# The first attention's context: halves made as rows, stored, and turned by the load from memory instead of by TensorE

## What is computed

```python
x = x + attention(layernorm(x), ctx)
def attention(query, ctx):
    q = query @ w_q.T + b_q
    k = ctx @ w_k.T + b_k
    v = ctx @ w_v.T + b_v
    scores = einsum('bhqd,bhkd->bhqk', q, k) / sqrt(16)
    y = einsum('bhqk,bhkd->bhqd', softmax(scores), v)
    return y @ w_o.T + b_o
```

## Time and profile before

| | us |
|---|---|
| median of 3 runs | 3887.06 (3885.37 to 3891.0) |
| the profiled execution | 3889.76 |
| its span in the profile | 3888.0 |
| TensorE busy | 3699.7 (95%) |
| VectorE busy | 3091.1 (80%) |
| ScalarE busy | 2208.8 (57%) |
| GpSimd busy | 2208.9 (57%) |
| first attention | from 23 to about 900 |
| granted clock over the span | 0.979 of 2.4 GHz |

### The profile page before, as it was taken

One profiled execution on the slowest core, in us unless ns is written; L12 is line 12 of the kernel. 1 busy time (PEld: TensorE's weight loads), 2 busy tenths in 40 slices (PEclk: granted clock), 3 DMA queues, 4 the chain that ended last, 5 costly groups with the idle time before them and its releaser, 6 DMA issues. The chain is left out here.

```text
span 3888.0 us, 134428 instructions
## 1 busy us (share of the span) xinstructions
PE 3699.7 (95%) x47408; PEld 2875.9 (74%) x47408; DVE 3091.1 (80%) x5266; ACT 2208.8 (57%) x4529; POOL 2208.9 (57%) x3316
## 2 busy tenths in 40 slices
PE   5999999994899999999999996899999989999999
PEld 4777777772677777777777775566666658888888
DVE  4888888886777777777777775799889877777777
ACT  3777777775444444444444442577767764555554
POOL 5666666663354533333333334366656667887777
PEclk9999999997899999999999998899999999999999
DMA  4677777765333322222222223699999962333332
GB/s 123 187 210 206 211 213 219 215 201 160 99 81 80 81 66 74 65 74 65 67 71 65 74 62 87 157 211 212 219 209 209 213 151 80 79 75 76 79 75 72
DMA packets 834241, 502.59 MB, mean 129 GB/s; under 512 B 262037, under 2 KB 824408, under 8 KB 833480
## 3 DMA queue, kind: packets, MB, share of 16 engines
q1 hardware_dynamic: 832680, 493.49, 50.3%
q0 software_dynamic: 928, 0.49, 0.1%
HBM read 251.27 MB, written 214.96 MB: 120 GB/s over the span
## 5 line engine op out<-in xcount | busy, mean ns | idle before, releaser
L1506 ACT ACTIVATE all_region<-phase_loop_hid,phase_b1T 128x128 f32<-128x128 f32 x2048 | 586.1, 368 | 728.0 <-PE phase_loop_hid L193 693.5
L191 PE MATMUL phase_loop_hid<-phase_loop_moe_h,phase_w_hi 128*128 128x128 f16 x4096 | 728.1, 220 | 0.1
L193 PE MATMUL phase_loop_hid<-phase_loop_moe_h,phase_w_lo 128*128 128x128 f16 x4096 | 726.4, 219 | 0.0
L192 PE MATMUL phase_loop_hid<-phase_loop_moe_h,phase_w_hi 128*128 128x128 f16 x4096 | 726.4, 219 | 0.0
L1112 DVE TENSOR_REDUCE phase_loop_mx<-phase_loop_score 128x8 f32<-128x1024 f32 x512 | 625.8, 1222 | 100.6 <-PE phase_loop_score L875 94.8
L1472 PE MATMUL phase_loop_moe_y<-phase_w,all_region 128*128 x2048 | 693.6, 379 | 0.3
L1030 ACT ACTIVATE phase_loop_pt<-phase_loop_scoreT 128x1024 f32<-128x1024 f32 x448 | 458.6, 1024 | 271.5 <-PE phase_loop_scoreT L909 269.2
L1474 PE MATMUL phase_loop_moe_y<-phase_w,all_region 128*128 x2048 | 558.2, 273 | 0.0
L1524 DVE TENSOR_SCALAR all_region<-all_region 128x512 f16<-128x512 f32 x512 | 257.6, 503 | 248.6 <-PE phase_loop_moe_y L1474 192.8
L191 PEld LDWEIGHTS phase_loop_hid<-phase_loop_moe_h,phase_w_hi 128*128 x4096 | 400.6, 98 | 66.5 <-issue 0.4
L1527 DVE SCALAR_TENSOR_TENSOR all_region<-all_region 128x512 f16<-128x512 f32 x512 | 410.1, 801 | 17.6
(11 more groups left out here) (276 smaller groups left out, 9846.6 us busy)
## 6 DMA issues: line engine op xcount, KB each, us to landing
qk_scratch<-phase_loop_qk SPq DMA_DIRECT2D x192, 256.0 KB, 3.5
phase_loop_qS<-qk_scratch SPq DMA_DIRECT2D x768, 64.0 KB, 3.2
phase_loop_cin<-in_ctx SPq DMA_DIRECT2D x128, 256.0 KB, 4.6
x_scratch<-phase_loop_x SPq DMA_DIRECT2D x128, 256.0 KB, 3.1
h_scratch<-phase_loop_hr SPq DMA_DIRECT2D x128, 256.0 KB, 3.8
phase_loop_kS<-qk_scratch SPq DMA_DIRECT2D x384, 64.0 KB, 2.4
ks_scratch<-ct_scratch SPq DMA_DIRECT2D x384, 64.0 KB, 2.4
phase_loop_kS<-ks_scratch SPq DMA_DIRECT2D x128, 192.0 KB, 3.9
```

The costliest lines, as they stand in the source:

```text
L191: eng.matmul(out, l_hi, r_hi, start=start, stop=False)
L192: eng.matmul(out, l_hi, r_lo, start=False, stop=False)
L193: return eng.matmul(out, l_lo, r_hi, start=False, stop=stop)
L1506: i = act.activation(hf[n % NF][:, j, :], hid(u, n)[:, j * S:(j + 1) * S], ACT.Gelu, bias=w["b1"][:, bass.ds(e * HB + (4 * half + j), 1)], ...
```

## The change

The context is no longer turned by TensorE. `hi_c` and `lo_c` now read `cin` in SBUF and write the halves side by side as rows into a new tile `cr`, of two buffers. `store_cr` writes them to a scratch tensor in memory, 256 KB per unit, and `load_cT` brings them back by one transposing load into `cT`. `kk` waits for that load in place of `lo_c`, and `store_ct` too. `t_c` is gone, from TensorE's list and from the plan of the PSUM bank. All tasks but those of the context get a lag larger by one, so the pipeline is one step deeper (DEPTH 13). In SyncE's list `load_c` and `store_cr` stand first and `load_cT` behind `store_h`.

The diff, cut to its core (the lists of GpSimd and ScalarE change in their lags alone):

```diff
-    DEPTH = 12
+    DEPTH = 13 if first else 12
...
+        cr = first and two("cr", [P, PAIR, 2, D], F16)
...
-            plan = [(3, "t_x"), (8, "t_y"), (3, "q"), (7, "y0"), (2, "t_c"), (3, "k"), (5, "t_max"), (3, "v"),
-                    (7, "y1"), (8, "o")]
-            shared = (("t_x", "y0", "y1"), ("t_y", "t_c", "t_max", "v"), ("q", "k", "o"))
+            plan = [(4, "t_x"), (9, "t_y"), (4, "q"), (8, "y0"), (4, "k"), (6, "t_max"), (4, "v"), (8, "y1"), (9, "o")]
+            shared = (("t_x", "y0", "y1"), ("t_y", "t_max", "v"), ("q", "k", "o"))
...
                 def load_c(u):
-                    (s_tc if first else s_ve).wait(sp, u.back(2))
+                    (s_cl if first else s_ve).wait(sp, u.back(2))
                     d_c.inc(sp.dma_start(cin[u.slot][:, :, :], cv[u.no]), u)
...
+                def store_cr(u):
+                    s_ch.wait(sp, u)
+                    s_cl.wait(sp, u)
+                    d_cr.inc(rows_out(sp, io["cr"][u.no], cr[u.slot][:, :, :, :]), u)
+
+                def load_cT(u):
+                    d_cr.wait(sp, u)
+                    s_k.wait(sp, u.back(2))
+                    s_v.wait(sp, u.back(4))
+                    d_ct.wait(sp, u.back(4))
+                    d_cT.inc(columns_in(sp, cT[u.slot4][:, :, :, :], io["cr"][u.no]), u)
...
                 def store_ct(u):
-
-                    s_cl.wait(sp, u)
-                    s_ch.wait(sp, u)
+                    d_cT.wait(sp, u)
...
-                    tasks = [(5, place_max), (3, stack_k), (2, store_q), (9, store_x1), (0, load_x), (4, store_ct),
-                             (4, store_max), (9, store_h), (0, load_c), (2, store_k), (2, stack_q)]
+                    tasks = [(0, load_c), (1, store_cr), (6, place_max), (4, stack_k), (3, store_q), (10, store_x1), (1, load_x),
+                             (5, store_ct), (5, store_max), (10, store_h), (1, load_cT), (3, store_k), (3, stack_q)]
...
-                def t_c(u):
-                    d_c.wait(pe, u)
-                    free("t_c", u)
-                    transpose_pair(pe, ring["t_c"], cin[u.slot], ident).then_inc(s_tc.sem, 1)
...
                 def kk(u):
-                    s_cl.wait(pe, u)
+                    d_cT.wait(pe, u)
...
                 def vv(u):
-                    s_cl.wait(pe, u)
...
-                    tasks = [(3, make["t_x"]), (8, make["t_y"]), (7, av(2)), (5, score(3)), (7, score_t(3)),
-                             (3, make["q"]), (7, make["y0"]), (2, make["t_c"]), (7, av(3)), (6, score_t(0)),
...
+                    tasks = [(4, make["t_x"]), (9, make["t_y"]), (8, av(2)), (6, score(3)), (8, score_t(3)),
+                             (4, make["q"]), (8, make["y0"]), (8, av(3)), (7, score_t(0)),
...
-                hi_c = first and hi_part(s_ch, ring["t_c"][:, :], cT, s_tc, [(s_v, 4), (d_ct, 4)], p2(CTX_X))
+
+                def hi_c(u):
+
+                    d_c.wait(act, u)
+                    d_cr.wait(act, u.back(2))
+                    act.activation(cr[u.slot][:, :, 0, :], cin[u.slot][:, :, :], ACT.Copy, scale=p2(CTX_X)).then_inc(s_ch.sem, 1)
...
-                lo_c = first and lo_part(s_cl, ring["t_c"][:, :], cT, 0, s_ch, [(s_v, 4), (d_ct, 4)], p2(CTX_X))
+
+                def lo_c(u):
+                    s_ch.wait(v, u)
+                    v.scalar_tensor_tensor(out=cr[u.slot][:, :, 1, :], in0=cin[u.slot][:, :, :], scalar=p2(CTX_X),
+                                           in1=cr[u.slot][:, :, 0, :], op0=ALU.mult, op1=ALU.subtract).then_inc(s_cl.sem, 1)
...
-                             (4, row_max(2)), (2, lo_x), (4, row_max(3)), (7, lo_y), (2, lo_q), (1, norm0_stats),
-                             (1, lo_c), (8, norm1_stats)]
+                             (5, row_max(2)), (3, lo_x), (5, row_max(3)), (8, lo_y), (3, lo_q), (2, norm0_stats),
+                             (1, lo_c), (9, norm1_stats)]
...
+        io["cr"] = nc.dram_tensor("cr_scratch", (n_seq // PAIR, PAIR * S, 2 * D), F16, kind="Internal").ap()
```

More of the change, by code:

```diff
@@ L531, in attention @@
         d_stq, d_stk = k.dsig("d_stq", 6), k.dsig("d_stk", 6 if first else 2)
-        d_ct = k.dsig("d_ct")
+        d_ct, d_cr, d_cT = k.dsig("d_ct"), k.dsig("d_cr"), k.dsig("d_cT")
         g = lambda name, per=1: k.sig(name, per)
-        s_tx, s_tc, s_xh, s_xl, s_ch, s_cl = g("s_tx"), g("s_tc"), g("s_xh"), g("s_xl"), g("s_ch"), g("s_cl")
+        s_tx, s_xh, s_xl, s_ch, s_cl = g("s_tx"), g("s_xh"), g("s_xl"), g("s_ch"), g("s_cl")
         s_q, s_k, s_v, s_qh, s_ql, s_kh, s_kl, s_ve = (g(n) for n in "s_q s_k s_v s_qh s_ql s_kh s_kl s_vev".split())
@@ L552, in attention @@
         read = {"y0": (s_yn, 1), "y1": (s_yn, 2), "t_y": (s_yl, 1), "o": (s_x1, 1), "t_max": (s_mte, 1),
-                "t_x": (s_xl, 1), "q": (s_ql, 1), "k": (s_kl, 1), "v": (s_ve, 1),
-                "t_c": (s_cl, 1)}
+                "t_x": (s_xl, 1), "q": (s_ql, 1), "k": (s_kl, 1), "v": (s_ve, 1)}
         ring, bank_of = {}, {}
@@ L789, in _ @@
                 if first:
-                    tasks = [(6, bias_x), (8, maxima), (5, norm0), (12, rstd1), (12, rows1)]
+                    tasks = [(7, bias_x), (9, maxima), (6, norm0), (13, rstd1), (13, rows1)]
                 else:
@@ L964, in o @@
                     project_rows(u, ring["o"], lambda u: yT[u.slot], "wo").then_inc(s_o.sem, 1)
-                make = {"t_x": t_x, "t_c": t_c, "q": q if first else fold_q, "k": kk, "v": vv, "t_max": t_max,
+                make = {"t_x": t_x, "q": q if first else fold_q, "k": kk, "v": vv, "t_max": t_max,
                         "y0": y_rows(0), "y1": y_rows(1), "t_y": t_y, "o": o}
                 if first:
-                    tasks = [(3, make["t_x"]), (8, make["t_y"]), (7, av(2)), (5, score(3)), (7, score_t(3)),
-                             (3, make["q"]), (7, make["y0"]), (2, make["t_c"]), (7, av(3)), (6, score_t(0)),
-                             (3, make["k"]), (5, make["t_max"]), (6, av(0)), (6, score_t(1)), (4, score(0)),
-                             (3, make["v"]), (7, make["y1"]), (6, score_t(2)), (4, score(1)), (8, make["o"]),
-                             (6, av(1)), (4, score(2))]
+                    tasks = [(4, make["t_x"]), (9, make["t_y"]), (8, av(2)), (6, score(3)), (8, score_t(3)),
+                             (4, make["q"]), (8, make["y0"]), (8, av(3)), (7, score_t(0)),
+                             (4, make["k"]), (6, make["t_max"]), (7, av(0)), (7, score_t(1)), (5, score(0)),
+                             (4, make["v"]), (8, make["y1"]), (7, score_t(2)), (5, score(1)), (9, make["o"]),
+                             (7, av(1)), (5, score(2))]
                 else:
@@ L1052, in _ @@
                 if first:
-                    tasks = [(5, copy_y(0)), (1, hi_x), (6, hi_y), (5, expo(3)), (1, hi_q), (0, hi_c), (5, copy_y(1)),
-                             (4, expo(0)), (3, copy_max), (1, hi_k), (4, expo(1)), (4, expo(2)), (1, copy_v),
-                             (7, norm1)]
+                    tasks = [(6, copy_y(0)), (2, hi_x), (7, hi_y), (6, expo(3)), (2, hi_q), (0, hi_c), (6, copy_y(1)),
+                             (5, expo(0)), (4, copy_max), (2, hi_k), (5, expo(1)), (5, expo(2)), (2, copy_v),
+                             (8, norm1)]
                 else:
@@ L1130, in _ @@
                 if first:
-                    tasks = [(7, norm_y(0)), (3, lo_k), (4, row_max(0)), (7, norm_y(1)), (4, row_max(1)), (8, add_x),
-                             (4, row_max(2)), (2, lo_x), (4, row_max(3)), (7, lo_y), (2, lo_q), (1, norm0_stats),
-                             (1, lo_c), (8, norm1_stats)]
+                    tasks = [(8, norm_y(0)), (4, lo_k), (5, row_max(0)), (8, norm_y(1)), (5, row_max(1)), (9, add_x),
+                             (5, row_max(2)), (3, lo_x), (5, row_max(3)), (8, lo_y), (3, lo_q), (2, norm0_stats),
+                             (1, lo_c), (9, norm1_stats)]
                 else:
```

## The result

The changed kernel takes **4336.16 us** (median of 4 runs, 4327.83 to 4337.39). The kernel before took 3888.39 on the same chip (4 runs, 3885.37 to 3891.0). The ratio is 1.1147 [1.1128, 1.1167]: 448 us slower, inside the range, 64 us under the predicted 4400. The profiled execution took 4327.8 us; its span is 4325.9, with TensorE busy for 3804.7 of it (88%) and VectorE for 3095.4 (72%).

A forecast was written before the change was run, and what follows sets the result against it. TensorE, busy for the whole 13.17 us step, was taken as the bound. A loop of 21.7 us per step gives 58 x (21.7 - 13.17) = 495, plus 12 and 6: +513 us, predicted 4400 us, range 4230 to 4520.

The forecast's parts named there:

- The removal: Four context transposes per unit leave TensorE, 0.53 us x 64 = 34 us; not subtracted because TensorE waits there instead.
- rival C: First attention: TensorE stays the bound and gives back 34 us, less 6 at the start: 3859 us; chance 0.03.
- The loop: First attention, steps 6 to 63: score_t(0), lo_c, store_cr and place_max wait in a circle, 21.7 us per step.
- TensorE from `score_t(0)` to the end of `score(3)`: Loop term: 9.93 us of consecutive TensorE work, plus 2.5 us lost to the low clock after the stop.
- VectorE to the end of `lo_c`: Loop term: row_max(3), lo_y, lo_q, the statistics and lo_c on VectorE, 4.85 us.
- The queue: Loop term on SyncE: waking, issuing store_cr, a gap and the two place_max transfers, 1.23 us.
- Landing of `place_max`: Loop term: from the end of its last issue until it lands, 3.2 us, bounds 1.9 and 4.36.
- the start: First load of x stands behind the context's store and both copies: +6 us once.
- the steps in which only `kS` is in the loop: Steps 4 and 5, before the first place_max: a shorter loop of 19.1 us, costing 6 us each.
- A: First attention: the loop closes but the clock stays up, 19.2 us per step, 4255 us; chance 0.15.
- B: First attention: no loop, but the queue or DMA engines become the bound, 14.2 us per step, 3953 us; chance 0.04.
- D: First attention: low clock through the whole step or landing of 4.4 us, about 4555 us; chance 0.07.

The follow-up runs named there:

- e3: The kernel before without the four transposes, context halves copied straight into cT, no store or load added, context not turned: 3879.81 us against 3883.28.
- e8: The changed kernel with 42 useless matmuls of 256 columns ahead of score_t(0)'s wait for place_max: 4211.21 us.
- e1: The changed kernel with the context's store and transposing load one step later, at the same places of the queue's list: 4006.06 us.
- e12: The changed kernel with the context's store and transposing load issued by ScalarE instead of SyncE's queue: 3979.54 us.
- e11: e1 with store_max and place_max issued by ScalarE instead of SyncE's queue: 3953.95 us.
- e10: e3 with store_max and place_max issued by ScalarE instead of SyncE's queue: 3892.51 us.
- e2: e1 with a plain load of the same 256 KB in place of the transposing one, context not turned: 3934.75 us.

## Why the prediction was right, and where it was off

**What bounds the kernel.** The judgement of the place was right: the slack of about 1 us between `place_max` and TensorE, and what stands in the queue ahead of it. The removal was rightly not subtracted, but its size was wrong even by itself: the 34 us that rival C was built on are 0 in e3. A busy share of 100% was read as the bound, and the next limits lie within 0.3 us of the step (12.95 against 13.17 in e3).

**The loop, term by term**, in the step of 20.48 us shown above:

- TensorE from `score_t(0)` to the end of `score(3)`: forecast 9.93 + 2.5 of low clock. Measured 411.52 - 398.93 = 12.59, so 2.66 of low clock. Confirmed, and by e8 too (at least 2.2 per step).
- VectorE to the end of `lo_c`: forecast 4.85, measured 416.29 - 411.52 = 4.77.
- The queue: forecast 1.23, measured 417.46 - 416.29 = 1.17.
- Landing of `place_max`: forecast 3.2, measured 419.41 - 417.46 = **1.95**. This is the term that was mis-sized. It came from the store of 256 KB ahead of it, taken at the 3.8 us of the like store of h. In the changed kernel that store lands sooner, as these two rows show (DMA issues from 200 to 1200: count, KB each, median us to landing):

```profile
cr_scratch<-phase_loop_cr SPq DMA_DIRECT2D x49, 256.0 KB, 2.2
...
phase_loop_cT<-cr_scratch SPq DMA_TRANSPOSE x49, 3.3
```

In e1, where the stop is gone, the same store lands in a median 4.2 us (300 to 600). So the very stop that the prediction described had left the DMA engines little to do (a share of 0.35 from 416 to 418, beside 0.87 in e1's window), and a landing time taken from the busy kernel was carried into an idle moment. The lower bound of 1.9, the shortest landing less the issue, was the right row. The difference is 1.25 us, x 58 = 73 us. That is nearly all of the 75 us by which the profiled execution lies under the forecast for it (4327.8 for 4403), and more than the 64 by which the median does.

Sum: the four terms give 12.59 + 4.77 + 1.17 + 1.95 = 20.48 for 21.7, in 58 steps as counted. By the starts of ScalarE's copies of the maxima the mean of these 58 steps is 20.39 us, and 13.25 in the kernel before, whose step the prediction took at 13.17 by a single one. So the loop cost 58 x (20.39 - 13.25) = 414 us for the 495 forecast. What stands ahead of them, the start and the steps in which only `kS` is in the loop, cost 22 us, where 6 + 12 were forecast: the first copy of the maxima starts at 74.03 for 65.08, and the second comes 26.7 us later for 13.5. Of this, 4.4 us are the first load of x, which goes out at 27.61 where it went out at 23.20.

```profile
27.61 0.46 SPq L600 DMA_DIRECT2D phase_loop_xin<-in_x  x1
```

**The rivals.** A, the clock stays up, gave 4255. The profile refutes it (behind each of the 58 stops from 100 to 1350 us the clock stands at 0.50, for 3.3 to 6.1 us and 5.7 in the mean), and e8, which is A made on purpose, took 4211: A's mechanism was real, its size too high by the same landing term: with 1.95 for 3.2 it gives 4255 - 73 = 4182, and the 29 us from there to e8 stay open. B, the queue or the DMA engines bind, is not what decides here, but it is what is left once the loop is opened: 3953 forecast, 4006 in e1, 3980 in e12, 3954 in e11. For both of its halves there are signs: relief of the queue is worth 52 us (e11 less e1), and with the queue relieved the DMA share is 0.96 to 0.99 and `qS` lands in 4.7 us for 2.8 (e12). How much each carries is not shown. C, faster, would have needed a gain from the transposes that e3 does not show. D, a low clock for the whole step or a landing of 4.4, didn't come.

**What stays open.** Why the freed step stops at 12.95 to 13.2 us isn't settled. TensorE's short waits for `lo_k` (0.17 us each in e3) and the expert weights' transfers were seen there, and e10 shows that without the queued maxima there are some 10 us in it. No run separates the two. Nor is it settled how e1's rest divides between a longer queue and busier DMA engines: a plain load with filler in the queue of the transposing load's length would tell. Nor was it tried to put `lo_c` earlier on VectorE, which would shorten the loop from the other side.

## What to carry to other kernels

When a transfer is put into an in-order queue, look up when its producer ends, not how long the transfer takes, and ask what is queued behind it. A load that lands in 2 us but goes out 5 us late closed a loop of all engines here: the change cost 448 us to take 34 us of work off TensorE, and one lag on two tasks was worth 330 of them. In the same way, count how long a transfer is in being issued, for a queue that is issuing nine tenths of the time may pay for it in every step (1.44 us beside 0.42, e1 and e2). And before work is taken off the busiest engine, run the kernel with that work simply left out: a busy share of 100% gave back nothing.

## What was not expected of the hardware

- Useless matmuls in the stop made the kernel faster by 125 us (4336 to 4211), with the clock at 0.99 instead of 0.84 (100 to 850 us). The wait ahead of `score_t(0)` was 5.04 us a step in the mean, and the low clock behind it cost 2.66 more in the step shown.
- A transposing load of 256 KB costs 1.1 us a piece more than a plain one where TensorE waits for neither (e1, e2). It holds the issuing queue for 1.44 us, the plain one for 0.42, and lands in 4.2 us for 3.5; the DMA engines move 212 GB/s at a share of 0.87 with it and 233 at 0.81 with the plain one.
- The same store (`cr`, 256 KB) lands in 2.2 us in the changed kernel, where it goes out in the stop (a share of 0.35 from 416 to 418), and in 4.2 in e1 (0.87 from 300 to 400). `qS` takes 2.7 us in the changed kernel (0.56) and 4.7 in e12 (0.99).
